# Second half of h stored from ScalarE's queue, three low parts of expert 1 moved up, tile 2 in two passes

## What is computed

```python
x = x + jnp.tanh(g_xattn[0]) * _L0_xattn_ref(_layernorm(x, axis=-1), ctx_4096)   # softmax(q k^T) k
x = x + jnp.tanh(g_ffn[0]) * _L0_ffn_ref(_layernorm(x, axis=-1), W_gate, b_gate, W_e, b_e)
# _L0_ffn_ref:
logits = x @ W_gate + b_gate
_, top_idx = jax.lax.top_k(logits, TOP_K)                     # TOP_K = 2, 8 experts
y_all = jax.nn.relu(jnp.einsum('bsd,edh->bseh', x, W_e) + b_e)
y = jnp.take_along_axis(y_all, top_idx[..., None], axis=2).mean(axis=2)
```

## Time and profile before

| | us |
|---|---|
| median of three executions | 343.05 |
| lowest, highest | 342.56, 344.18 |
| the profiled execution | 344.42 |
| its span, from the first to the last instruction | 342.5 |
| PE busy | 319.5 (93%) |
| VectorE (DVE) busy | 203.9 (60%) |
| ScalarE (ACT) busy | 122.9 (36%) |
| GpSimd (POOL) busy | 75.3 (22%) |

### The profile page before, as it was taken

One profiled execution on the slowest core, in us unless ns is written; L12 is line 12 of the kernel. 1 busy time (PEld: TensorE's weight loads), 2 busy tenths in 40 slices (PEclk: granted clock), 3 DMA queues, 4 the chain that ended last, 5 costly groups with the idle time before them and its releaser, 6 DMA issues.

```text
span 342.5 us, 4328 instructions
## 1 busy us (share of the span) xinstructions
PE 319.5 (93%) x1510; PEld 235.1 (69%) x1510; DVE 203.9 (60%) x434; ACT 122.9 (36%) x165; POOL 75.3 (22%) x91
## 2 busy tenths in 40 slices
PE   5699999999999999959999999999999999999970
PEld 5344565565665588738788888888888888888850
DVE  2324457676668886886694975755176575753220
ACT  2223434625534558013345535515032551431000
POOL 6000110100103320303334321530120333011120
PEclk9969999999999999999999999999999999999995
DMA  7999999999948799567999999998359989634152
GB/s 253 303 288 303 349 353 332 354 319 362 389 156 292 268 382 327 147 225 206 379 340 367 353 355 354 255 381 273 61 169 346 282 215 382 208 61 63 10 84 31
DMA packets 24711, 90.57 MB, mean 264 GB/s; under 512 B 3276, under 2 KB 3276, under 8 KB 24680
## 3 DMA queue, kind: packets, MB, share of 16 engines
q1 hardware_dynamic: 13752, 52.86, 43.6%
q0 software_dynamic: 7792, 25.47, 28.5%
q10 hardware_dynamic: 3136, 11.83, 10.4%
HBM read 73.63 MB, written 16.52 MB: 263 GB/s over the span
## 4 chain that ended last, share of the span: by engine, by line
PE 80%; DMA 10%; DVE 4%; POOL 1%; ACT 1%; issue 1%; SPq 0%; DVEq 0%
PE ps L449 49%; PE ps L357 11%; PE ps L382 11%; DMA hn_rows<-hn 4%; PE ps L432 4%; DMA wg<-in_L_ffn_W_gate 3%; DMA xg<-hn_rows,src_token 2%; PE ps L403 2%; PE ps L394 1%; PE ps L348 1%; DVE stats L738 1%; DVE x_all L789 1%; DMA x_all<-in_x 1%; PE ps L365 1%; POOL guess L1117 1%
## 5 line engine op out<-in xcount | busy, mean ns | idle before, releaser
L449 PE MATMUL ps<-wh,xh 128*128 128x512 f32 x256 | 83.0, 400 | 0.1
L449 PE MATMUL ps<-wl,xh 128*128 128x512 f32 x256 | 80.4, 393 | 0.3 <-issue 0.3
L881 DVE TENSOR_TENSOR wl<-raw,wh 128x1024 fp32r<-128x1024 f32 x64 | 75.6, 1219 | 8.4 <-ACT wh L632 8.1
L449 PE MATMUL ps<-wh,xl 128*128 128x512 f32 x256 | 80.2, 393 | 0.0
L632 ACT ACTIVATE wh<-raw 128x1024 fp32r<-128x1024 f32 x64 | 63.7, 1051 | 22.9 <-DMA raw<-in_L_ffn_W_e 20.9
L449 PEld LDWEIGHTS ps<-wl,xh 128*128 128x128 f32 x256 | 48.0, 188 | 11.4 <-DVE wl L881 0.7
L449 PEld LDWEIGHTS ps<-wh,xl 128*128 128x128 f32 x256 | 48.0, 188 | 10.7
L449 PEld LDWEIGHTS ps<-wh,xh 128*128 128x128 f32 x256 | 46.4, 188 | 9.3 <-DVE xl L885 0.5
L1065 POOL DMA_INDIRECT out_rows<-y,dst_token x15 | 29.0, 1933 | 107.1 <-DVE y L895 88.5
L635 ACT ACTIVATE xh<-ps 128x1024 fp32r<-128x1024 f32 x16 | 16.4, 1024 | 90.1 <-PE ps L432 90.1
L357 PE MATMUL ps<-kT,qT 128*100 128x361 f32 x128 | 43.4, 493 | 1.0 <-ACT qT L611 1.0
(11 more groups left out here) (124 smaller groups left out, 240.0 us busy)
## 6 DMA issues: line engine op xcount, KB each, us to landing
raw<-in_L_ffn_W_e SPq DMA_DIRECT2D x64, 512.0 KB, 9.2
kT<-in_ctx_cols SPq DMA_DIRECT2D x16, 722.0 KB, 11.3
ctx<-in_ctx ACTq DMA_DIRECT2D x8, 1024.0 KB, 11.1
bias<-in_L_ffn_b_e SPq DMA_DIRECT2D x8, 512.0 KB, 10.9
ctx<-in_ctx ACTq DMA_DIRECT2D x8, 420.0 KB, 14.5
hn_rows<-hn POOLq DMA_DIRECT2D x8, 400.0 KB, 9.5
out_rows<-x_all POOLq DMA_DIRECT2D x2, 1600.0 KB, 19.1
x_all<-in_x SPq DMA_DIRECT2D x7, 384.0 KB
```

What stands on the lines that cost most here:

```text
L449: mm = nc.tensor.matmul(into[:, n * HB:(n + 1) * HB], rows[:, k, :], weights[:, k, n * HB:(n + 1) * HB], start=(k == 0 and c == first), st ...
L881: nc.vector.tensor_tensor(wl[e % 2][:, k, :], raw[e % 2][:, k, :], wh[e % 2][:, k, :], ALU.subtract).then_inc(s_wl, 1)
```

## The change

The second half of h is no longer stored by GpSimd behind the last `hn` store. ScalarE issues it in its own queue, after it has normalised batch 7. Each half has a semaphore of its own. VectorE makes the low parts k = 0 and 1 of expert 1 ahead of the last `locate`, and k = 2 ahead of `name_tokens`. TensorE does tile 2 in two passes: HH and HL for all k, waiting only for the high rows, with `s_wfree` raised after each k and the turn of tile 3 after k = 5; then LH for all k, which raises a new semaphore, `s_wh0free`. ScalarE waits for this before it overwrites `wh` of expert 0 with expert 2's. On GpSimd the wait for the h stores stands ahead of the first overflow gather.

```diff
             sp.wait_ge(s_hn, B)
-            sp.wait_ge(s_hstore, 16 * len(STORES))
+            for h in range(HALVES):
+                sp.wait_ge(s_hstore[h], 16)
             load_bias(0)
...
+                if n == 2:
+
+                    pe.wait_ge(s_xh, n + 1)
+                    for k in range(KD):
+
+                        tile(n, k, (HH, HL), None).then_inc(s_wfree, 1)
+                        if k == 5:
+                            turn_tile(n + 1)
                 pe.wait_ge(s_xl, n + 1)
...
-                    mm = tile(n, k)
+                    mm = tile(n, k, (LH,)) if n == 2 else tile(n, k)
                     if half == 1:
-                        mm.then_inc(s_wfree, 1)
+                        mm.then_inc(s_wh0free if n == 2 else s_wfree, 1)
                     if n + 1 < N_TILES:
-                        if k == 2:
+                        if k == 2 and n > 2:
                             turn_tile(n + 1)
...
             def split_weights(e, k):
                 act.wait_ge(s_raw[e % 2][k], 16 * (e // 2 + 1))
+                if e == 2:
+                    act.wait_ge(s_wh0free, k + 1)
...
             normalise_hidden(B - 1)
+
+            act.wait_ge(s_h, B)
+            act.dma_start(*hidden(*STORES[1])).then_inc(s_hstore[1], 16)
             split_tile(1)
...
             split_tile(1)
+
+            split_weights(1, 0)
+            split_weights(1, 1)
             locate(B - 1)
+            split_weights(1, 2)
             name_tokens(1)
-            for k in range(KD):
+            for k in range(3, KD):
                 split_weights(1, k)
...
                 store_normed(s - 1)
-                if s == B:
-                    store_hidden(*STORES[1])
                 if s + 1 == B:
 
-                    store_hidden(*STORES[0])
+                    pool.wait_ge(s_h, HALF_B)
+                    g.dma_start(*hidden(*STORES[0])).then_inc(s_hstore[0], 16)
...
+            for h in range(HALVES):
+                pool.wait_ge(s_hstore[h], 16)
             gather_first_over(0, over, over_before)
-
             pool.wait_ge(s_zero, 32)
-            pool.wait_ge(s_hstore, 16 * len(STORES))
             add_tile(0)
```

More of the change, by code:

```diff
@@ L227, in gated_block @@
         s_table = sem("tile_table_ready")
-        s_hstore = sem("h_stored")
+        s_hstore = [sem(f"h_stored{h}") for h in range(HALVES)]
         s_hnstore = sem("hn_stored")
@@ L233, in gated_block @@
         s_wfree = sem("w_used")
+        s_wh0free = sem("first_w_high_used")
         s_gath = [sem(f"gathered{t}") for t in range(2)]
@@ L265, in gated_block, with hidden @@
         STORES = ((0, HALF_B), (HALF_B, B))
+        def hidden(first, end):
+            return out[first * Q:end * Q, :].rearrange("(b q) d -> q b d", q=Q), x_all[:, first:end, :]
         FIRST_CHUNKS = {3: (0,), 4: (1,), 5: (2,), 6: (3,), 7: (4, 5), 8: (6, 7)}
@@ L647, in wait_multiplied @@
                 else:
-                    eng.wait_ge(s_wfree, KD * (e + 1))
+                    eng.wait_ge(s_wh0free if e == 0 else s_wfree, KD if e == 0 else KD * (e + 1))
             def split_over(over_before, j):
@@ L902, in evacuate @@
                 else:
-                    dve.wait_ge(s_wfree, KD * (e + 1))
+                    dve.wait_ge(s_wh0free if e == 0 else s_wfree, KD if e == 0 else KD * (e + 1))
                 dve.wait_ge(s_bias[e % 2], 16 * (e // 2 + 1))
@@ L959, in _ @@
             split_tile(2)
-            dve.wait_ge(s_hstore, 16 * len(STORES))
+            for h in range(HALVES):
+                dve.wait_ge(s_hstore[h], 16)
             dve.wait_ge(s_hn, B)
@@ L1043, in _ @@
             pool.nop().then_inc(s_const, 1)
-            def store_hidden(first, end):
-                pool.wait_ge(s_h, end)
-                rows = out[first * Q:end * Q, :].rearrange("(b q) d -> q b d", q=Q)
-                g.dma_start(rows, x_all[:, first:end, :]).then_inc(s_hstore, 16)
             def store_normed(b):
```

## The result

| | before | after |
|---|---|---|
| median of six executions each, us | 342.85 | 347.12 |
| lowest, highest | 340.76, 344.18 | 345.42, 348.38 |
| the profiled execution | 344.42 | 348.38 |
| its span | 342.5 | 346.5 |

The ratio is 1.0108, with a 95% interval of 1.007 to 1.0145: slower by 4.3 us in the medians and by 4.0 us in the spans. The forecast was 351.2 us (340.8 to 354.0). The direction is right, and the loss is half of what was forecast.

A forecast was written before the change was run, and what follows sets the result against it. The prediction took TensorE's work from the start of tile 2 to bound the kernel. From the median 343.05 us, +5.7 (store) - 0.3 (gather) - 0.3 (low rows) + 3.1 (clock) = +8.2 gave 351.2 us, range 340.8 to 354.0.

The forecast's parts named there:

- What bounds the kernel: Tiles 2 to 15 are fixed TensorE work, so whatever moves the start of tile 2 moves the end equally.
- The hn store, +5.7 us: Last `hn` store, ahead of tile 2's gather: lands 5.7 us later, the middle of 5.1 and 6.3, sharing engines with h.
- The ten engines: Store of h on ScalarE's queue: spread over ten engines only, 8.2 us instead of 5.7; not in the sum.
- The gather, -0.3 us: Gather of tile 2: no longer behind h in its queue, so 0.3 us shorter (bounds 0 and 1.0).
- The low parts: Three low parts in VectorE's gaps: tokens slip about 0.2 us, hidden by the `hn` store; alone worth next to nothing.
- Tile 2 in two passes, -0.3 us: Start of tile 2: the wait for the low rows falls away, 0.3 us gained.
- The clock, +3.1 us: TensorE's hole ahead of tile 2: clock falls to half speed, 6.24 us of work lose 3.1 us (bounds 0 and 3.4).
- The sum: Whole kernel: store, gather, low rows and clock add up to +8.2 us, giving 351.2 us.
- no collision: Rival: queues don't get in each other's way, `hn` store still lands at 141.76; 341.8 to 342.8 us; chance 0.18.
- earlier landing: Rival: `hn` store lands earlier, tokens decide, 2.8 us faster, 340.3 us; chance 0.16.
- a slip of 1 to 5 us with no fall of the clock: Rival: store slips but the clock holds, or h spreads well; 343.5 to 347.5 us; chance 0.10.
- The biases: SP's queue: their 1 MB may run beside the `hn` store, 0 to 3.3 us more; taken as 0.

The follow-up runs named there:

- e4_fill: The whole change, with 46 transposes of the identity ahead of the turn of tile 2 so that TensorE isn't idle; ratio 1.0057.
- e11_gate_g4: As e9_gate, with the gather of tile 4 issued ahead of the add of tile 0; 343.15 us, ratio 0.9982.
- e16_half_hold: The whole change, ScalarE storing only batches 4 and 5 of h, and biases held until the last `hn` store has landed; ratio 1.0007.
- e3_spread: The whole change, with ScalarE's store of h cut into 96 and 4 partitions so that all 16 engines carry it; ratio 1.0101.
- e15_spread_hold: As e3_spread, with the biases held back until the last `hn` store has landed; ratio 1.0134.
- e1_queue_only: The kernel before, with only the second half of h moved to ScalarE's queue; 346.95 us, ratio 1.0119.
- e6_late: The whole change, but ScalarE issues the second half of h only once the last `hn` store has landed; ratio 1.0107.
- e2_rest_only: The whole change, but with the second half of h stored by GpSimd as in the kernel before; ratio 0.9983.
- e7_half: The whole change, with ScalarE storing only batches 4 and 5 of h, batches 6 and 7 left out; ratio 1.0111.
- e5_early: The kernel before, with the first half of h and the zeros issued right behind the first two gathers; 352.98 us, ratio 1.0273.
- e8_early_rest: As e5_early, with the low parts in the gaps and tile 2 in two passes added; 348.38 us, ratio 1.0143.
- e9_gate: The whole change, but ScalarE issues h after tile 2's gather lands; biases, first evacuation and first two adds wait only for h's first half; 344.74 us, 1.0023.
- e13_later: As e11_gate_g4, but ScalarE issues the second half of h only after its own register loads; 346.27 us, ratio 1.0101.
- e14_software: As e11_gate_g4, but GpSimd issues the second half of h, right after the gather of tile 2; 344.37 us, ratio 1.0055.

## Why the prediction was right or wrong

**What bounds the kernel: right.** All 4.0 us arose ahead of tile 2, and tiles 2 to 15 took the same time. In e4_fill and e11_gate_g4 too it is 178.4 us from the start of tile 2 to the last matmul, wherever that start is.

**The hn store, +5.7 us: right that it slips, wrong in its price.** It slipped by 4.0 us (18.88 - 15.23 = 3.65, and 0.3 by a later issue), below both ends between which I took the middle. The step that failed is the sentence that h "can't stand ahead of the `hn` store" in the kernel before. 1.3 of its 1.64 MB did. The whole price of h for that store is 18.88 - 11.65 = 7.2 us, and the kernel before already paid 15.23 - 11.65 = 3.6 of it. I derived a full price for bytes from the order of issue. The trace of before could have told that q0 moves 4.02 MB in the flight of the store. But a price from bytes alone would then have been 1.2 us for the 0.34 MB that are new, too little by 2.5. That h costs more from a queue of its own is shown (e16_half_hold, the changed kernel); by what means is open. Neither price comes out at 4.0.

**The ten engines: rightly left out of the sum.** "DMA: Bandwidth & Descriptors" of the Trainium skill says, in "Why a DMA increments its semaphore by 16 and not by 1", that a copy of 100 partitions issued in a hardware queue goes over ten engines. The trace agrees: the semaphore of h is raised 11 times in the changed kernel, and 21 times with the pieces of 96 and 4 partitions, which by that section is once for each engine and once for the rest (10 + 1, and 16 + 4 + 1). The 2.5 us more that I worked out from it did not come, and with all 16 engines (e3_spread, e15_spread_hold) the store takes 19.9 and 19.1 us instead of 18.9. The engines of h are not what the `hn` store waits for.

**The gather, -0.3 us: wrong in size, and its bounds too narrow.** It fell by 1.5 us (7.33 to 5.81), more than my end of 1.0, though its instruction was held up for 1.4 us. In other runs it took 4.59 (e1_queue_only) to 10.90 us (e6_late), by what lay beside it. The bound came from one gather in another stretch. The prediction did not see that VectorE can hold GpSimd up.

**The low parts: right that they are worth nothing.** The tokens came 0.3 us later (140.37), where I had 0.2, behind the store's landing.

**Tile 2 in two passes, -0.3 us: wrong.** The sum took the wait for the low rows as what held the start of tile 2. It was not: TensorE's second pair of register loads ended at 152.9 in the kernel before, 0.1 us ahead of the start, and I had counted only the first pair. At a granted clock of 1.00 tile 2 starts 3.68 and 3.75 us after its turn (e2_rest_only, e4_fill), where I had 3.3 and the kernel before 3.58. In the medians this and the low parts together can't be seen (0.9983).

**The clock, +3.1 us: right in kind, twice too large.** It fell in the hole and stayed low for 6.83 us, as at the start of the kernel; TensorE was at work for 5.94 us of it, of which 0.77 fall in tile 2 and leave nothing to see in its later stretch. From turn to tile 2 it cost 1.4 to 1.5 us (5.17 against 3.75 and 3.68), and e4_fill gained 1.7 us in the medians. I had counted each busy microsecond at half speed as half lost. But at the slow clock the register loads are done while the eight low products run, so that the stops which they make at 1.00 (0.30 and 0.2 us in e4_fill) are not there.

**The sum.** Forecast 5.7 - 0.3 - 0.3 + 3.1 = 8.2 us; shown 4.0 - 1.5 for the arrival of the gathered rows, +0.1 for the low rows, +1.5 for the clock: 4.1 us, with rounding. Too much were 1.7 us for the store, 1.2 for the gather and 1.6 for the clock, too little 0.4 for the low rows. The rivals "no collision" and "earlier landing" fell with the landing at 145.73. The one that was nearest in size, a slip of 1 to 5 us with no fall of the clock (343.5 to 347.5 us), had a chance of only 0.10; it was wrong on the clock. The biases hardly mixed in (issued at 144.25), but do so where h is done sooner (e3_spread, e7_half).

**Could it have been better than before?** No run shows it. Beside the `hn` stores the stores of h leave TensorE 3 to 6 us of wait (both kernels, e5_early, e8_early_rest), beside the gather 5.6 us (e6_late), beside the register loads 2.5 us (e9_gate), and with h after that 3 to 4 us in several stops (e13_later, e14_software), one of them without a known cause. The best, e11_gate_g4, ends level with the kernel before.

**What stays open.** Why h costs the `hn` store more from a queue of its own than from the same queue, and on which engines that store ends. Why some gathers issued within a run of low parts are held to its end and others are not. In the traces those not held started 0.86 to 0.97 us behind the start of a low part, and no held one did, but no run tests this. Two gathers of tile 3 (the kernel before, 1.87 us, and e5_early, 1.88) ended well within their run of five. What TensorE waits for in e14_software ahead of tile 3. And how the register loads are slowed: the runs show when, not through what.

## What to carry to other kernels

A transfer issued behind another in the same software queue need not be behind it on the engines: take the bytes that the queue moved during the flight of the critical transfer, before you price a move to another queue. And test the move by itself, for the same bytes can cost another time from there. When the stretch ahead of a critical DMA is full of bytes that must be moved anyway, moving the issue moves the loss to the next thing in flight, and here even to register loads. A hole that grows in TensorE can be priced twice, once as idle time and once as low clock behind it. And before you take away the wait that ends last, look at what ends just before it: here the next release, by register loads, came at the same time.

## What the runs showed of the hardware that was not expected

- The software queue did not serve its transfers one after the other: 1.3 MB of the store issued second moved before the first had landed, and taking the second away shortened the first from 15.2 to 11.7 us.
- A gather's instruction on GpSimd takes about 1 us alone and up to 4.37 us when it meets VectorE's run of three subtractions of two float32 operands; in seven such cases it ended 0.8 to 0.93 us after the run. In nine traces it met a run of two or five and took only 1.20 to 1.28 us. The Trainium skill, "SBUF — State Buffer", section "SBUF: two separate sides", has a lock between the two engines for VectorE instructions with two inputs in SBUF against a GpSimd instruction that reads SBUF, held for the whole instruction. The seven cases agree with it; the nine others it doesn't explain. Its section "A bandwidth-pool intuition that's wrong (but worth ruling out)" gives about 0.115 us from the end of VectorE's instruction, there a copy, to the end of the wait; here the gather's instruction ended 0.8 to 0.93 us after the run.
- A register load from `tile_table` in SBUF has no fixed cost: mostly 0.3 to 0.55 us, but 0.9 to 2.1 us in e9_gate, e11_gate_g4 and e13_later while 1.6 MB are being stored from ScalarE's queue. With the store in GpSimd's queue (e14_software) it is 0.3 to 0.85 us.
- Spreading a competing store over all 16 engines raised the rate from 130 to 135 us (1.01 instead of 0.74 of the engines, 330 instead of 288 GB/s), and did not bring the other queue's store in sooner.
